# Values projected in the FFN stage and kept in DRAM; attention's query and key chunks in every second round

## The reference

```python
xn = _layernorm(x, axis=-1)
q = xn @ Wq;  k, v = jnp.split(xn @ Wkv, 2, axis=-1)        # 16 heads of 64
q, k = _rope(q), _rope(k)                                   # on the first 32 of the 64
attn = softmax(q @ k.T * DIM_HEAD ** -0.5)                  # per head
a = (attn @ v) @ Wout + bout
h = silu(fp4_linear(xn, w_gate)) * fp4_linear(xn, w_up)     # 704 wide, blocks of 16
out = x + a + fp4_linear(h, w_down)                         # fp4_linear quantises both operands
```

## Time and profile before

| | us |
|---|---|
| median of three runs | 2085.81 |
| the profiled execution | 2086.47 |
| its span, first to last instruction | 2084.4 |
| PE busy | 1888.5 (91%) |
| DVE busy | 1556.3 (75%) |
| POOL busy | 1516.5 (73%) |
| ACT busy | 826.0 (40%) |
| mean granted clock of PE, as a share of 2.4 GHz | 0.974 |

### The profile page before, as it was taken

The page is one execution under the profiler, slowest core; times in us unless marked ns, Lnnn a source line. Parts: engine busy times, 40 slices in busy tenths (PEclk is TensorE's granted clock), DMA queues, the critical chain, the costliest instruction groups (busy, mean ns, idle before and its releaser), DMA issues. The chain is left out here.

```text
span 2084.4 us, 30067 instructions
## 1 busy us (share of the span) xinstructions
PE 1888.5 (91%) x11300; PEld 1198.1 (57%) x11300; DVE 1556.3 (75%) x1967; ACT 826.0 (40%) x1068; POOL 1516.5 (73%) x699
## 2 busy tenths in 40 slices
PE   1288989669999999999999999999999999999499
PEld 0277888435555555555555555555555555555299
DVE  8699999467777777777777777777777777775154
ACT  1222332114444444444444444444444444444232
POOL 2356555218888888888888888888888888888444
PEclk9999999869999999999999999999999999999799
DMA  8100101300111121111112111111211111101286
GB/s 295 50 31 33 56 33 58 114 21 26 46 33 42 50 69 37 52 32 47 42 37 82 32 47 32 54 34 47 80 39 42 32 47 32 32 27 32 95 291 212
DMA packets 132282, 129.80 MB, mean 62 GB/s; under 512 B 40880, under 2 KB 96816, under 8 KB 132016
## 3 DMA queue, kind: packets, MB, share of 16 engines
q1 hardware_dynamic: 132144, 127.96, 19.4%
HBM read 87.56 MB, written 40.37 MB: 61 GB/s over the span
## 5 line engine op out<-in xcount | busy, mean ns | idle before, releaser
L1046 POOL TENSOR_TENSOR acc<-acc,prob 128x1024 f32<-128x1024 f32 x384 | 939.0, 2445 | 154.2 <-ACT prob L1089 125.8
L927 DVE TENSOR_REDUCE half_max<-m_ps 128x2 f32<-128x1024 f32 x512 | 625.4, 1221 | 340.2 <-PE m_ps L800 337.7
L1089 ACT ACTIVATE prob<-s_ps 128x1024 f32<-128x1024 f32 x512 | 498.4, 1025 | 362.0 <-PE s_ps L824 278.2
L839 PE MATMUL o_ps<-prob,v 128*64 128x512 f32 x2048 | 492.5, 602 | 0.0
L839 PEld LDWEIGHTS o_ps<-prob,v 128*64 128x64 f32 x2048 | 130.0, 136 | 250.8 <-issue 183.7
L1028 POOL TENSOR_TENSOR turned<-straight,shuffled 128x512 f32<-128x512 f32 x128 | 191.5, 1496 | 82.5 <-DVE shuffled L959 82.5
L800 PE MATMUL m_ps<-k_hi,q_hi 64*128 64x512 f32 x1024 | 233.3, 451 | 16.7 <-DVE half_max L927 14.4
L869 PE MATMUL misc_ps<-xT,wqk 128*128 128x512 f32 x768 | 219.2, 422 | 18.3 <-DMA xT<-xn_scratch 10.8
L869 PEld LDWEIGHTS misc_ps<-xT,wqk 128*128 128x128 f32 x768 | 138.9, 194 | 143.6 <-issue 109.0
L821 PE MATMUL s_ps<-q_hi,k_hi 64*128 64x512 f32 x1024 | 203.8, 393 | 0.0
L821 PE MATMUL s_ps<-q_lo,k_hi 64*128 64x512 f32 x1024 | 202.4, 390 | 0.0
(11 more groups left out here) (126 smaller groups left out, 2419.7 us busy)
## 6 DMA issues: line engine op xcount, KB each, us to landing
wqk<-wp_scratch SPq DMA_DIRECT2D x32, 512.0 KB, 4.1
inv_rows<-inv_scratch SPq DMA_DIRECT2D x128, 128.0 KB, 2.9
o_scratch<-o_norm SPq DMA_DIRECT2D x64, 256.0 KB, 2.0
o_in<-o_scratch SPq DMA_DIRECT2D x8, 2048.0 KB, 10.8
xn_scratch<-xnT SPq DMA_DIRECT2D x8, 1024.0 KB, 4.3
xT<-xn_scratch SPq DMA_DIRECT2D x8, 1024.0 KB, 5.8
wv<-wp_scratch SPq DMA_DIRECT2D x32, 256.0 KB, 3.5
wp_scratch<-wp_hl SPq DMA_DIRECT2D x8, 768.0 KB, 4.0
```

Source lines behind the costliest of these rows:

```text
L839: ins = nc.tensor.matmul(o_ps[head * DH:(head + 1) * DH, :], v[s // 2 % 2][:, kt, s % 2, at:at + DH], prob[n % SLOTS][:, head, :], start=k ...
L927: nc.vector.tensor_reduce(half_max[:, half % 2, :, t % GRP, part], m_ps[:, :, :], axis=AX.X, op=ALU.max, negate=True).then_inc(half_maxed, 1)
L1046: nc.gpsimd.tensor_tensor(acc[b][:, :, :], first, prob[n % SLOTS][:, :, :], ALU.add).then_inc(added, 1)
L1089: nc.scalar.activation(prob[n % SLOTS][:, :, :], s_ps[n % 2][:, :, :], ACT.Exp).then_inc(exp_done, 1)
```

## The change

The value weights are split once, whole (`wv`, 128 x 2 x 2048), in the weights part, and stay in SBUF through the FFN part. There, PE multiplies each tile of the normalised input with them, half of the 1024 columns between the gate and the up product and half after the up product, both into `down_ps`, the bank of the down product. ACT copies each half to SBUF, and SP stores each tile's values to DRAM. In the attention part each step loads its values from there; the value jobs of rounds 6 and 7 and their copies on ACT are gone, and the chunks go from rounds 1, 2, 3, 5 to 1, 3, 5, 7. `WP` falls from 3 x 128 to 2 x 128 columns.

```diff
+            sp.dma_start(wv_in[:, :], io["wv"]).then_inc(wv_loaded, 16)
+            pool.wait_ge(wv_high, 1)
+            nc.gpsimd.tensor_tensor(wv[:, LO, :], wv_in[:, :], wv[:, HI, :].bitcast(F32), ALU.subtract)
+            act.wait_ge(wv_loaded, 16)
+            nc.scalar.activation(wv[:, HI, :], wv_in[:, :], ACT.Copy).then_inc(wv_high, 1)
...
+            def copy_v(g, t, k):
+                n = g * GRP + t
+                act.wait_ge(v_mult, n * 2 + k + 1)
+                if k == 0 and not (type(n) is int and n < 2):
+                    act.wait_ge(v_stored[t % 2], 16 * (g * 2 + t // 2))
+                nc.scalar.activation(v_out[t % 2][:, k * 512:(k + 1) * 512], down_ps[:, :], ACT.Copy).then_inc(v_copied, 1)
...
                     if t + 1 < GRP or ahead(g, 1):
+                        copy_v(g, t + 1, 0)
                         silu(n + 1)
+                        copy_v(g, t + 1, 1)
                     if ahead(g, 1):
                         high_x(n + GRP, t)
...
+            def project_v(n, t, k):
+                if k:
+                    pe.wait_ge(v_copied, n * 2 + 1)
+                elif not (type(n) is int and n < 4):
+                    pe.wait_ge(res_ready, n - 3)
+                elif n:
+                    pe.wait_ge(v_copied, n * 2)
+                i = 0
+                for xs, ws in PARTS:
+                    for c in range(DC):
+                        ins = nc.tensor.matmul(down_ps[:, :], xnT[:, t, xs, c, :], wv[:, ws, c * INNER + k * 512:c * INNER + (k + 1) * 512],
+                                               start=i == 0, stop=i == 3 * DC - 1)
+                        i += 1
+                ins.then_inc(v_mult, 1)
...
                 for w, ps in enumerate((gate_ps, up_ps)):
+                    if w:
+                        project_v(n, t, 0)
...
                 ins.then_inc(gate_up, 1)
+                project_v(n, t, 1)
...
             def down(n):
                 pe.wait_ge(h_high, n + 1)
+                pe.wait_ge(v_copied, min(n * 2 + 8, 2 * TILES) if type(n) is int else n * 2 + 8)
...
+                    if more or t + 3 < GRP:
+                        at = n + 3
+                        if type(n) is not int:
+                            at = sp.snap(at)
+                        store_v(at, n + 3, t + 3)
                     if more and t == GRP - 2:
                         store_x(g + 1)
...
-CHUNK_ROUND = {1: K0, 2: K1, 3: Q0, 5: Q1}
+CHUNK_ROUND = {1: K0, 3: K1, 5: Q0, 7: Q1}
...
+                    if r == 0 and scoring(s + 1):
+                        rotate(s + 1, Q1)
                     if r - 1 in CHUNK_ROUND and scoring(s + 2):
                         rotate(s + 2, CHUNK_ROUND[r - 1])
...
+                    if r == 1 and scoring(s + 1):
+                        low(s + 1, Q1)
...
+            def load_v(s):
+                if s >= 2:
+                    sp.wait_ge(pv_done, (s - 1) * UNITS)
+                at = s // PAIRS * QT
+                sp.dma_start(v[s % 2][:, :, :], io["v_scratch"][at:at + QT, :, s % PAIRS * P:(s % PAIRS + 1) * P]
+                             .rearrange("t p n -> p t n")).then_inc(v_loaded[s % 2], 16)
```

More of the change, by code:

```diff
@@ L41 @@
 QT = SEQ // P
-WP = 3 * P
+WP = 2 * P
 GRP = 4
@@ L351, in ffn_part @@
     res = sb("res", [P, 2, D], F32)
+    v_out = [sb(f"v_out{i}", [P, INNER], F32) for i in range(2)]
     turn = psum("turn", [P, 2 * 512], F32)
@@ L367, in ffn_part @@
     x_all, mean, rstd, ident = kept["x_all"], kept["mean"], kept["rstd"], kept["ident"]
-    wgT, wdT = kept["wgT"], kept["wdT"]
+    wgT, wdT, wv = kept["wgT"], kept["wdT"], kept["wv"]
+    v_mult, v_copied, v_stored = sem("v_mult"), sem("v_copied"), [sem(f"v_stored{i}") for i in range(2)]
     def groups(eng, group):
@@ L668, in _ @@
             store_x(0)
+            for n in range(3):
+                store_v(n, n, n)
             with sp.Fori(0, NG - 1) as g:
@@ L720, in attention_part @@
     wqk = [sb(f"wqk{i}", [P, 2, DC, 2 * P], F32R) for i in range(2)]
-    wv = [sb(f"wv{i}", [P, 2, DC, 2, P], F32R) for i in range(2)]
     q_hi = [sb(f"q_hi{i}", [P, SEQ], F32R) for i in range(3)]
@@ L725, in attention_part @@
     k_lo = [sb(f"k_lo{i}", [P, SEQ], F32R) for i in range(3)]
-    v = [sb(f"v{i}", [P, QT, 2, P], F32) for i in range(2)]
+    v = [sb(f"v{i}", [P, QT, P], F32) for i in range(2)]
     crossed = [sb(f"crossed{i}", [P, GCOL], F32) for i in range(2)]
@@ L831, in values @@
                 pe.wait_ge(exp_done, n + 1)
-                if u == 0 and s % 2 == 0:
-                    pe.wait_ge(v_done, 4 * (s // 2 + 1))
+                if u == 0:
+                    pe.wait_ge(v_loaded[s % 2], 16 * (s // 2 + 1))
                 if kt == 0 and 2 * s + half:
@@ L1051, in _ @@
                         add_tile(s * UNITS + 2 * r)
+                    if r == 0 and scoring(s + 1):
+                        add_rotated(s + 1, Q1)
                     if r - 1 in CHUNK_ROUND and scoring(s + 2):
@@ L1135, in load_wqk @@
                              io["wp_scratch"][s % PAIRS].rearrange("p h (c n) -> p (h c) n", c=DC)[:, :, 0:2 * P]).then_inc(wqk_loaded[s % 2], 16)
-            def load_wv(group):
-                if group >= 2:
-                    sp.wait_ge(misc_done, job["v", 2 * group - 3, 1] + 1)
-                for j in range(2):
-                    sp.dma_start(wv[group % 2][:, :, :, j, :].rearrange("p h c n -> p (h c) n").bitcast(F32),
-                                 io["wp_scratch"][(2 * group + j) % PAIRS].rearrange("p h (c n) -> p (h c) n", c=DC)[:, :, 2 * P:3 * P]).then_inc(wv_loaded[group % 2], 16)
+            def load_v(s):
[4 more added lines that the diff above has]
+                             .rearrange("t p n -> p t n")).then_inc(v_loaded[s % 2], 16)
             def load_x(b, half):
                 if b:
-                    last = job["chunk", b * PAIRS - 1, Q0] if half == 0 else job["v", b * PAIRS - 1, 1]
+                    last = job["chunk", b * PAIRS - 1, Q0 if half == 0 else Q1]
                     sp.wait_ge(misc_done, last + 1)
@@ L1203, in _ @@
                     load_x((s + 3) // PAIRS, 1)
-                group = (s + 5) // 2
-                if s % 2 and group >= 2 and 2 * group < STEPS:
-                    load_wv(group)
+                if scoring(s + 4) and s + 4 >= 2:
+                    load_wqk(s + 4)
             for b in range(2):
@@ L1372, in build @@
             hold("wdT", [P, FT * D], F32)
+            hold("wv", [P, 2, DC * INNER], F32R)
             part(weights_part)
```

68 lines of the change are left out of this document (25 added, 43 removed).

## The result

The kernel after the change takes 2111.31 us (median of four runs, 2107.86 to 2114.36) against 2085.87 before: a ratio of 1.0119, 95% interval 1.0100 to 1.0137. It is 1.2% slower; 2113 us was forecast. The profiled execution took 2111.92 us, with a span of 2110.1 where it was 2084.4.

A forecast was written before the change was run, and what follows sets the result against it. The prediction took PE to bound attention and DVE the FFN part. Its terms: FFN +76.6, attention steps -47, step 30 +2.5, attention start -6.5, weights +1, sum +26.6 on 2086.47: 2113 us, range 2074 to 2142.

The forecast's parts named there:

- PE takes over the FFN part: FFN tiles: two value groups of 3.16 us and a 0.33 us copy wait make PE the bound, 11.02 us per tile.
- The store of x: FFN part: ACT waits for the store issued behind the values; PE waits 2.1 us in six groups, 12.6 us.
- The first tile: FFN start: the first tile has its two groups before the second gate product, partly at half clock, +4 us.
- The tail: FFN end: the last silu and a PE list still behind come later by +3.5 us.
- the start of the attention part: Before the first guess: two value jobs are gone, so the guess comes some 6.5 us earlier.
- The attention steps: Full steps: 43.74 us of PE's list, +0.94 for rotations, +0.73 for o_norm behind q_lo: 45.41 us; 30 steps, -47 us.
- Step 30 and the end: Last attention step: two waits on DVE without the covering chunk in round 1, +2.5 us.
- The weights part: Before the FFN part: ends 3 us earlier or 4 later, by where DVE's last products fall between POOL's splits; +1 taken.
- A: Attention part: DVE hides everything, a step takes 43.9 us, -93 instead of -47, 2067 us in all; chance 16%.
- B: FFN part: the new waits don't appear, 22 us less, 2091 us in all; chance 9%.
- C: Attention part: POOL or a chain through it takes over, a step takes 46.5 us, 2146 us in all; chance 12%.
- D: Value products run at the page's gap (216 ns), 18 us less, 2095 us in all; chance 3%.

The follow-up runs named there:

- e4: Changed kernel with the transposes of h ahead of the down product in PE's list, plus a wait for ACT's copy: 2106.93 us.
- e3: Changed kernel with the store of x issued ahead of the store of values in SP's list: 2096.44 us.
- e6: Changed kernel with the values' low-part products left out, two products per group instead of six: 2073.16 us (one run).
- e2: Changed kernel with o_norm of the first half moved on DVE from round 1 to round 2: 2079.14 us.
- e1: Changed kernel with the chunks back in rounds 1, 2, 3 and 5, values still computed in the FFN part: 2068.22 us.
- e5: Changed kernel with o_norm in round 2, the store of x first and the transposes of h ahead of the down product: 2049.69 us.
- e7: Changed kernel with chunks in rounds 1, 2, 3, 5, the store of x first and the transposes of h ahead of the down product: 2036.59 us.
- e8: Changed kernel with o_norm ahead of q_lo, the last chunk's split, in round 1: 2108.48 us (one run).

## Why the prediction was right, and where its sizes were off

The forecast was slower by 1.3%, and 1.2% was measured, by the mechanisms named. That the totals are 1 us apart (+26.6 and +25.74) is partly luck, since two errors cancelled: the FFN part was forecast 5 us too dear (+76.6, measured +71.57), and the gain of the attention part 5 us too large (-51.0, measured -45.79). Term by term:

**PE takes over the FFN part: right.** A tile was forecast at 11.02 and took 10.86 us. Two sizes in it were off against each other. A group of six products takes 1.40 us, not the 1.58 of a chunk: 28 tiles x 0.36 = 10 us too much. Chunks in the attention part still take 1273.29 - 1271.70 = 1.59 us, so a row of the same shape from another stage is not the same price. The single products of the two rows show why 1.58 / 6 = 263 ns was a wrong reading. In the FFN part they start 0.23 us apart. In the chunk the first two start 0.34 us apart, the next four 0.23 each, and the next guess comes 0.32 after the last. The extra 0.19 us lie at the chunk's two ends. Its neighbours there are products with weights of another shape (128*64 before it, 64*128 after it); in the FFN part the neighbours have 128*128 too. That the change of shape is the cause was not tried. By the Trainium skill's formula for one product (TensorE: Matmul & The Clock Gate, Back-to-back issue gap) a group would be 1.30 us, an estimate; the 1.40 lies between that and my row. The wait for the copy was forecast at 0.33 and is 0.46, 28 x 0.13 = 4 us too little; e4 shows it is a wait that other work fills. PE's share of 33.81 / 36 = 94% is just under the 95% that I had named as a sign, since a tile with a store of x lies in that stretch.

**The store of x: right in place, low in size.** ACT waited for it six times, and PE behind `res` each time. I had 6 x 2.1 = 12.6 us; e3 shows 16.2. Four waits cost 1.57 us, under the forecast. The first two cost 5.0 each: PE waited 3.17 and 3.12 us, as the stores landed later, and then ran 3.4 us at half clock, for 1.55 us more. The prediction had no term for the clock. Why the first two stores land later than the other four was not settled. That a wait of this kind does not get shorter with PE's list was not in the prediction either; e4 and e6 showed it: ACT waits 5.8 to 5.9 us there too, for every store that lands as fast.

**The first tile: too high.** +4 was forecast for its two groups, +1.13 came. The groups take 1.50 and 1.40 us, at full clock. The rest between the start of the up product and the second gate product fell from 102.35 - 98.66 = 3.69 us to 103.43 - 100.11 - 1.40 = 1.92: PE's wait of 0.94 us there is gone, and the clock, full from 100.1 us on before and from 98.8 after, no longer slows the start of the up product. The tail (+3.06 for +3.5) and the start of the attention part (-6.37 for -6.5) were right.

**The attention steps: right in mechanism, 0.26 us too long each.** A step takes 45.67 us, 45.41 was forecast. The rotations in rounds 0, 4 and 6 make them 4.79, 4.77 and 4.79 us (4.78 forecast). Round 2 was forecast at 4.78 + 0.73 = 5.51 and took 5.72: the mis-sized term is "+0.73" for the two neighbours on DVE, which measures 5.72 - 4.78 = 0.94 here, and 0.97 per step in e2. I let the maximum of round 2 start 0.7 us late; it started 0.96 late, 1.50 us after its product where the first maximum of round 1 starts 0.54 after. Over 29 steps this is 6 of the 6.6 us by which the saving fell short.

**Step 30 and the end:** +0.9 with the step's own saving, +0.53 measured.

**The weights part: left undecided, and now seen to have two outcomes.** The first gate product comes at 94.94 us in the kernel after and 94.6 to 95.7 in e1, e4 and e6, but at 91.6 to 91.8 in e2, e3, e5, e7 and e8, whose weights parts are the same. In the early runs only the last of the three DVE operations on `y` and `wd` below is held long by one of POOL's subtractions; in the late runs two of the three are. DVE and POOL in the kernel after:

```profile
51.53 4.75 DVE L119 TENSOR_TENSOR y<-y,m 128x1536 f32<-128x1536 f32 x1
...
57.53 4.73 DVE L120 TENSOR_TENSOR y<-y,m 128x1536 f32<-128x1536 f32 x1
...
62.30 1.76 DVE L121 TENSOR_TENSOR wd<-y,scale 128x1536 f32<-128x1536 f32 x1
```

And in e3, where it is the earlier trace rows again:

```profile
53.83 5.93 DVE L121 TENSOR_TENSOR wd<-y,scale 128x1536 f32<-128x1536 f32 x1
```

In the first, two of the three operations take 4.7 us; in the second only the last is held up that long before `wd` is ready, which comes at 59.76 instead of 64.06. It is worth about 3 us at the first gate product. e5 and e7, both early, came in 4 and 3 us under what I expected from late runs, which would fit. One execution of each kernel was profiled, four late and five early, so how much of the spread between runs it makes stays open.

**The rivals.** A (DVE hides everything, a step of 43.9) did not happen in this kernel: 45.67. But its time is real: with the chunks' old rounds the step is 44.13 (e1, e7), within 0.4 us of PE's list. I had looked for it in the new order, and took some 2 us for the split in the old order's bare round for granted, where 0.78 came; that is why e1 came in 22 us under the low end of what I expected. B (no new waits in the FFN part) is what the edits of e3 and e4 make of it together: 335.09 to 303.97 us. It was possible, but not in the order as written. C (POOL takes over) did not come: POOL is busy for 320.45 of 368 us, and PE waits for DVE, not for a chunk. D (the page's gap, 216 ns) was wrong for the chunks, and more than half right for the FFN part: 1.40 is 0.18 of the 0.28 us below 1.58.

## What to carry to other kernels

Two changes made at once are two forecasts: here moving work to a stage with free time gained 1%, and the regrouping of what was left behind lost 2%. Where an engine waits for a DMA that is issued behind its own work, the whole latency is exposed, and a shorter list on another engine does not shorten it; look at what a new store is put in front of. An idle wait of PE can cost more than its length: look at the granted clock behind it before you put the whole loss down to the wait. Of two neighbouring DVE operations that read SBUF beside a busy POOL, the second is the dear one, since it starts with a whole POOL operation still ahead of it: put a maximum or another operation on PSUM between them, as e2 did.

## What the runs showed of the hardware that was not expected

- Six products of 512 columns take 1.40 us in the FFN part and 1.59 in the attention part, both at a granted clock of 1.00. Inside both groups the products start 0.23 us apart; the difference lies at the first and the last product of the group, 0.1 us each. Eight products fewer (e6) are 1.87 us of PE's work, again 0.233 each.
- A `q_lo`, `k_lo` or `o_norm` (two inputs in SBUF) that started while POOL computed ended 0.55 us after POOL's operation, in each of the 184 cases of the kernel after, so its duration went from 0.76 to 2.90 us by its start alone. The addition that POOL started in between took 2.66 us, the one before it 2.35. Two neighbours on DVE took 4.63 us together and 4.65 in the other order, from the start of the first to the end of the second.
- PE's granted clock fell to half for 3.4 us behind waits of 3.17 and 3.12 us in the kernel after, and behind the 4.07 of the kernel before. In e4 it fell behind three of the four waits of 1.82 to 1.88 us and, for 6.9 us, behind one of 3.69, but not behind one of 2.62; in e6 behind waits of 1.33 to 2.85 with one for `h` after them. A stretch of 3.4 us cost 1.55 us. With the waits gone (e3, e5, e7) it stayed at 1.00 from the second gate product to the last.
- Behind a store of 512 KB, a store of 1 MB let ACT go on 5.05 us after its issue (290.05 to 295.10), where it took 4.45 before. For the first such store it was 6.9 us (148.24 to 155.13), with ACT waiting 7.69.
